# A softmax in groups of four: the value products of a group issued in one block behind the fourth score of the next group

## The reference

```
q = _apply_rope(_rms_norm(x @ wq.T)) / sqrt(8);  k likewise;  v = x @ wv.T
scores = jnp.einsum('bqhd,bkhd->bhqk', q, k)
attn = jax.nn.softmax(scores.astype(jnp.float32), axis=-1)
out = jnp.einsum('bhqk,bkhd->bqhd', attn, v).reshape(b, s, HIDDEN)
return out @ wo.T
```

## Time and profile before

| | |
|---|---|
| median of 3 runs | 1927.39 us (1926.84 to 1927.91) |
| the profiled execution's own time | 1925.29 us |
| its span in the trace | 1923.6 us |
| PE busy over the span | 1677.3 us (87%) |
| DVE busy over the span | 1590.5 us (83%) |
| ACT busy over the span | 1428.0 us (74%) |
| first and last L1643 (64 of them) | 628.1 and 1869.5 us |

### The profile page before, as it was taken

How to read it: one execution, slowest core, us unless ns; L and a number is a source line. 1 busy time by engine, 2 the same in 40 slices (tenths; PEclk the granted TensorE clock), 3 DMA queues, 4 the chain that set the end, 5 groups by cost and what they waited for, 6 DMA issues and landing times. The chain is left out here.

```text
span 1923.6 us, 41668 instructions
## 1 busy us (share of the span) xinstructions
PE 1677.3 (87%) x15983; PEld 703.1 (37%) x15983; DVE 1590.5 (83%) x2881; ACT 1428.0 (74%) x2861; POOL 319.8 (17%) x668
## 2 busy tenths in 40 slices
PE   4992888753598999999999999999999999999997
PEld 4552763253496222222222222222222222222224
DVE  3660444758855999999999999999999999999982
ACT  2111546533442799999999999999999999999997
POOL 2273006616210000000000000000000000002221
PEclk9795998857798899999999999999999999999999
DMA  8014112121221001101001010010110101101001
GB/s 264 13 54 122 42 43 57 48 88 43 55 47 42 1 4 16 19 2 19 7 13 18 2 19 10 10 19 1 19 15 5 19 2 18 18 2 29 13 15 53
DMA packets 64294, 61.82 MB, mean 32 GB/s; under 512 B 10752, under 2 KB 52736, under 8 KB 64096
## 3 DMA queue, kind: packets, MB, share of 16 engines
q1 hardware_dynamic: 57952, 46.56, 10.8%
q0 software_dynamic: 6144, 12.60, 2.2%
HBM read 23.21 MB, written 22.94 MB: 24 GB/s over the span
## 5 line engine op out<-in xcount | busy, mean ns | idle before, releaser
L1638 DVE TENSOR_REDUCE at_tops<-bank 128x1 f32<-128x512 f32 x2048 | 1233.1, 678 | 14.6 <-PE bank L1496 9.0
L1597 ACT ACTIVATE experts_then_probs<-bank 128x512 f32<-128x512 f32 x2048 | 1093.5, 600 | 73.3 <-PE bank L1516 52.9
L1516 PE MATMUL bank<-queries,keys 64*128 64x512 bf16 x2048 | 630.8, 383 | 44.4 <-ACT experts_then_probs L1597 38.3
L1496 PE MATMUL bank<-keys,queries 64*128 64x512 bf16 x2048 | 655.8, 388 | 5.1 <-POOL at_shift L1409 4.3
L1532 PE MATMUL bank<-experts_then_probs,values 128*32 128x256 f32 x8192 | 640.8, 390 | 0.0
L1516 PEld LDWEIGHTS bank<-queries,keys 64*128 64x128 bf16 x2048 | 128.4, 93 | 501.8 <-ACT experts_then_probs L1597 413.5
L1532 PEld LDWEIGHTS bank<-experts_then_probs,values 128*32 128x32 f32 x8192 | 167.6, 108 | 309.9 <-ACT experts_then_probs L1597 206.5
L1428 POOL CAST at_shift<-at_neg 128x8 bf16<-128x8 f32 x64 | 14.0, 218 | 1109.5 <-DVE at_neg L1643 1109.5
L1496 PEld LDWEIGHTS bank<-keys,queries 64*128 64x128 bf16 x2048 | 148.7, 93 | 65.9 <-DVE at_tops L1638 50.7
L653 DVE COPY ep_weights<-WB 128x642 f32 x72 | 35.7, 496 | 88.7 <-DVE ep_slots L664 46.5
L1589 ACT ACTIVATE queries<-bank 3x512 bf16<-3x512 bf16 x128 | 75.4, 589 | 32.4 <-PE bank L1506 29.3
(11 more groups left out here) (253 smaller groups left out, 1522.4 us busy)
## 6 DMA issues: line engine op xcount, KB each, us to landing
queries<-operand_parts SPq DMA_DIRECT2D x192, 32.0 KB
keys<-operand_parts SPq DMA_DIRECT2D x192, 32.0 KB
sorted_pairs<-zeros SPq DMA_DIRECT2D x16, 288.0 KB, 3.3
ep_slots<-sorted_pairs SPq DMA_DIRECT2D x6, 768.0 KB, 9.2
made_of_pairs<-ep_slots SPq DMA_DIRECT2D x6, 768.0 KB, 4.1
sorted_tokens<-zeros SPq DMA_DIRECT2D x8, 312.0 KB, 3.4
x<-in_L_attn_x_dram SPq DMA_DIRECT2D x4, 512.0 KB, 6.0
experts_then_probs<-in_L_ffn_W_dram SPq DMA_DIRECT2D x1, 2048.0 KB, 9.2
```

Source lines behind the costliest of these rows:

```text
L1496: mm = nc.tensor.matmul(bank[:, unit_bank(u) + a % WIDE, :], queries[pair % 2][rows, at:at + P], keys[pair % 2][rows, kb * CHUNK:(kb + 1) ...
L1516: nc.tensor.matmul(bank[:, bank_of("score", n, s), :], keys[pair % 2][rows, at:at + P], queries[pair % 2][rows, c * CHUNK:(c + 1) * CHUNK] ...
L1597: nc.scalar.activation(probs[:, s % PR, :], bank[:, bank_of("score", n, s), :], ACT.Exp).then_inc(p_ready, 1)
L1638: nc.vector.tensor_reduce(tops[:, m % 2, h * TPC + qt, kb // WIDE:kb // WIDE + 1], bank[:, at:at + WIDE, :].rearrange("p b n -> p (b n)"), ...
```

## The change

In the loop on TensorE, a group was weighed in two halves, one behind the second score of the next group and one behind its fourth (for group 0 of a chunk both behind the fourth). Now both halves of every group stand behind the fourth score.

```
--- before.py
+++ after.py
                     g = s // G - 1
-                    if s % G == 1 and g:
+                    if s % G == 3:
                         weigh(n, g, 0)
-                    if s % G == 3:
-                        if g == 0:
-                            weigh(n, g, 0)
                         weigh(n, g, 1)
```

## The result

The changed kernel takes 2002.43 us (median of 4 runs, 2000.55 to 2003.75) against 1927.12 us before: a ratio of 1.0392, 95% interval 1.0374 to 1.0410. The forecast was 1997 us (1983 to 2009).

The account below looks back on a forecast made before the run. DVE bounded the kernel; after the change, five groups of 2.40 us plus 3.12, 2.90 and 2.80 make a chunk 20.82 us, +1.13. Over 62 chunks that adds 70 us, giving 1997 us (1983 to 2009).

Parts of the forecast that it names:

- DVE was the bound: In the softmax stage, DVE's reductions set the pace: 2.39 us for a group of four against PE's 2.22.
- The loop of 2.40 us: Each group on PE: score reaching ACT 0.43, exponential freeing its bank 0.65, step to block 0.32, block 1.00 us.
- The excesses: Over 2.40 us: s = 8-11 (transposed sums) 0.72, s = 24-27 (shifts) 0.50, s = 28-31 (shift copies) 0.40.
- The sum: A chunk's groups total 20.82 us against 19.69, +1.13; over 62 chunks with maxima beside their scores, +70 us.
- The sums' copy costs nothing: On ACT in group 0, the copy of the sums was costed at nothing, or 0.1 us if late.
- PE's saved time counts for nothing: Rival denied here: fourth score does not wait, a group takes PE 2.01 us, DVE stays the bound, 1916 us; 4%.
- DVE does not stop PE: Rival denied here: after a chunk's end PE's fourth maximum waits for a bank, adding 25 us: 2022 us; 4%.
- ACT's idle time: ACT idle for about 0.47 us in most groups: 2.40 less four spacings of 0.48.

Follow-up runs that it names:

- the run with single waits: Changed kernel with the sums' wait on the copied sums and the shifts' wait on the split maxima moved ahead of their groups' third score: 1999.17 us, ratio 1.0380.

## Why the prediction was right

- *DVE was the bound, with 0.17 us a group to spare on PE.* Right: with the last block split, the chunk falls to DVE's 19.51, the 19.50 that the prediction gave as its floor.
- *The loop of 2.40 us.* Right to 0.01 us in the profile after. That it is a loop was shown by shortening two of its terms, the block and the exponential, by closing it through the other ring, and by moving the block. Its other two terms, 0.43 and 0.32, were only read from the rows.
- *The excesses.* Predicted 0.72, 0.50 and 0.40 us for the three long groups. The sums' group is 3.19 us instead of 3.12. The shifts' group has the same 0.74 us ahead of its shifts and is 2.97 (1301.37 to 1304.34 on PE) instead of 2.90; the group behind it is 2.75 (to 1307.09) instead of 2.80, so these two together are long by 0.02 only. The term that was mis-sized is "the bank is free at 0.92 + 0.65 = 1.57", which holds for a score but not for an instruction with a second wait: 0.74 in place of 0.65, shown by the run with single waits.
- *The sum.* 1.13 us a chunk predicted, 1.21 measured; 62 chunks make 75 us instead of 70. Of the difference of 0.08, the sums' group is 0.07; with single waits a chunk is 20.84 us, where 20.82 was forecast. The last two chunks, which the prediction put at some 2 us at most, took 2.6 more in the profiled execution.
- *The sums' copy costs nothing.* Right: the packets of ACT on both sides of it are 2.40 us apart.
- *PE's saved time counts for nothing.* Right: over the whole span PE is busy for 1634.4 us instead of 1677.3 with the same instructions, and the kernel is slower. The shorter bare time was real, and it lay beside the path.
- *DVE does not stop PE.* Right: PE's weight loads for the maxima wait for DVE 4 times in the stretch, 1.1 us in all, where they waited 106 times before.
- *ACT's idle time.* Put at 0.47 us a group from spacings of 0.48, which would give 0.48; with the spacing of 0.49 it is 0.44, and 0.33 + 0.11 = 0.44 was measured. Nothing else hangs on it.

## What to carry to other kernels

On an in-order engine, work that does not feed the waiting engine should not stand in one piece directly behind an instruction that waits for a buffer: the buffer's round trip and the whole piece then add up (here 1.08 + 0.32 + 1.00 us a group), and this costs as soon as the sum is longer than what the bound engine needs for the same work (2.39). Put part of the piece ahead of that instruction, where it runs under the wait. To find such a place, walk the ring once: which earlier instruction frees the buffer, and what lies between the two on the engine; and compare the walk's length, rather than the busy times, with the engine that is the bound.

## What the runs showed of the hardware

In the changed kernel the transposed sums and the shifts, which wait for two semaphores, started 0.73 to 0.74 us behind the start of the late exponential, in each of the 63 chunks whose loop has them; with the wait for that exponential alone they started 0.64 to 0.65 us behind it, as the scores do in both kernels. That is 0.09 us for the second wait, which was not expected of a condition that had long been met. Moving that wait to an earlier instruction with slack takes it away. What the engine does in the 0.09 us, the runs do not show.
